# Attention probabilities sent through memory: the rearranging moved from the load to the store

## The chip, the cores and the metric

One core of a Trainium2 chip runs the whole program. The metric is the device time of one execution in microseconds, lower is better.

## What is computed

The reference is a gated block on x (4 sequences of 512 tokens, width 1024) with a context of 4 x 64 keys. First cross attention: x is normalised, queries are formed with Wq (32 heads of 128), keys and values from the context (8 key/value heads), both rotated by position, and

    attn = softmax(mask(q k^T * 128**-0.5));  x = x + tanh(g_xattn) * (attn v) Wd^T

Then a quantised feed-forward of inner width 512 (gate, up, down) with its own gate is added. Everything in the attention is float32 work; operands of TensorE are split in a high and a low part, and three products take the place of one.

The part that the change touches is the transposed copy of the probabilities: for each batch row and pair of heads, P (tokens x keys) has to become P^T (keys x tokens), so that TensorE can contract over the keys.

## The kernel before

**Tiling.** The batch is worked in two halves of two sequences. In a half there are 8 groups (one key/value head each) of 4 units; a unit is one pair of heads on one sequence, so there are 32 units in a half and 64 in all. TensorE's order is written out by hand in slots, one slot per unit (L652). In the slot of unit u it computes the queries of u in eight parts (`queries`), the scores of unit u-1 (`score`), some of the products of Wd with the values (`values`, eight per group) and some of the sixteen `outputs` of the group before, which multiply P^T (`pt_hi`, `pt_lo`) with those products (`vw_hi`, `vw_lo`). The slots of a group are called kind 0 to 3 (u modulo 4). `outputs(gg, 0)` is the first to need P^T of the group's unit of kind 2; it stands in the slot of kind 0 of the next group.

**The probabilities.** VectorE subtracts the row maximum of the scores into `prob` (L1438, `softmax_a`), ScalarE takes the exponential in place (L959), VectorE sums, scales and transposes `prob` in blocks of 32 x 32 (L1444 to L1455, `softmax_b`). After that the 32 x 32 blocks are right inside, but stand in the wrong places. For all units but the last two of each half (`moved`, L294: 30 per half, 60 in all) the blocks are put in place by a trip through memory, `move_probs` (L451), issued by the sync engine (SP):

- one store of `prob`, 128 rows of 2 KB, to one of two halves of `p_dram`, laid out (a, q, t, c, i): a is the block row and q the row in it (together the partition), t one of four token tiles, c the block column (32 keys), i the column in it;
- a wait for it (L457), and a wait until `pt_raw`, which has one buffer, was read by VectorE for the unit before (L459);
- four loads (L461), one for each c, into 32 partitions of `pt_raw` each. Memory has 32 consecutive floats for each (q, t, a), so such a load is made of 512 pieces of 128 bytes.

ScalarE copies `pt_raw` to `pt_hi` (L944, `copy_probs`) and VectorE forms `pt_lo` (L1317 with `lower_probs`, L1457). There is one `prob` buffer: the subtraction for unit u+1 waits until the store of unit u has landed (L1435).

**What stands around it on each engine.** The order on each engine is fixed. SP in the slot of kind 3, after the move of the unit of kind 2: a piece of Wd (`next_wd`, L424), then in the next slot a pair of Wq (four transfers, L358), Wd, keys, Wd, values. VectorE in a slot of kind 0: rotation of the queries before (`turn_second`), `lower_values`, `lower_probs(unit - 2)`, `softmax_a(unit - 1)`, `lower_values`, the first half of the rotation (`turn_first`, L1413, which frees the bank of PSUM that the next slot's queries need), two additions of outputs, `softmax_b(unit - 1)`. ScalarE in that slot: values, a piece of Wd, `copy_probs(unit - 2)`, `exponential(unit - 1)`, values.

Of the kernel before, what the change touches and what calls it, by code (L numbers as in the profile page):

```python
# [46 lines left out]
BT = SEQ // P  # L47
# [40 lines left out]
def gated_block(nc, x, ctx_t, g_att, g_ffn, wq_t, wk_t, wv_t, wd_t, wg_t, wu_t, wo_t,  # L88
# [4 lines left out]
    p_dram = nc.dram_tensor("p_scratch", (2, 4, 32, BT, 4, 32), F32, kind="Internal").ap()  # L93

    root = ExitStack()
    with root:
        def sem(name):
            return root.enter_context(nc.semaphore(name))

        def sb(stack, name, shape, dt):  # L100
            return stack.enter_context(nc.sbuf_tensor(name, [P] + shape, dt))
# [38 lines left out]
        with ExitStack() as s:  # L140
# [8 lines left out]
            prob = sb(s, "prob", [2 * BT, KEYS], F32)  # L149
# [18 lines left out]
            pt_raw = sb(s, "pt_raw", [BT, 4, 32], F32)  # L168
# [62 lines left out]
        turned_done, p_out = sem("turned_done"), sem("p_out")  # L231
        pt_in = [sem("pt_in0"), sem("pt_in1")]
# [61 lines left out]
        def moved(unit):  # L294

            return unit % UNITS < UNITS - 2

        def moves(unit):

            return unit + 1 - 2 * (unit // UNITS)  # L300

        def turns(unit):

            return unit % UNITS - (UNITS - 2) + 1 + 2 * (unit // UNITS)
# [24 lines left out]
        def _(sp):  # L329
# [121 lines left out]
            def move_probs(unit):  # L451

                n = moves(unit)
                sp.wait_ge(turned_done, n)
                sp.dma_start(p_dram[n % 2, :, :, :, :, :].rearrange("a q t c i -> (a q) (t c i)"),
                             prob[:, :, :].rearrange("p s k -> p (s k)")).then_inc(p_out, 16)
                sp.wait_ge(p_out, 16 * n)  # L457
                if unit:
                    sp.wait_ge(pt_lo_done, unit)  # L459
                for c in range(4):  # L460
                    sp.dma_start(pt_raw[32 * c:32 * c + 32, :, :, :],  # L461
                                 p_dram[n % 2, :, :, :, c, :].rearrange("a q t i -> q t a i")).then_inc(pt_in[n % 2], 16)

            load_k(0)
            load_v(0)
            for half in range(HALVES):
                for u in range(UNITS):
                    unit, gg = half * UNITS + u, half * GROUPS + u // UPG
                    if u % 2 == 0 and 1 < unit // 2 + 1 < HALVES * PAIRS and unit != UNITS:
                        sp.wait_ge(q_done, unit)  # L470
                        load_wq(unit // 2 + 1)
                    if u % UPG == 0 and u >= UPG:
                        next_wd(VPG * gg - 2)
                        next_heads(gg)
                        next_wd(VPG * gg - 1)
                        next_values(gg)
                    if u % UPG == 1 and half == 0:
                        sp.wait_ge(part_done, HTILES + u // UPG)
                        sp.dma_start(xn[:, :], x[HTILES + u // UPG, :, :]).then_inc(xs_in, 16)
                    if u % UPG == 2:  # L480
                        next_wd(VPG * gg)
                        next_wd(VPG * gg + 1)
                    if u % UPG == 3:
                        for i in range(2, 5):
                            next_wd(VPG * gg + i)
                    if u >= 1 and moved(unit - 1):
                        move_probs(unit - 1)
                    if u % UPG == 3:
                        next_wd(VPG * gg + 5)
                    if half == 1 and 1 <= u <= 5:  # L490
                        load_again(((0, 1), (2, 3), (4,), (5, 6), (7,))[u - 1])
# [391 lines left out]
        def _(act):  # L883
# [50 lines left out]
            def copy_probs(unit):  # L934
                p, b, gg = (unit // HB) % 2, unit % HB, unit // UPG
                if gg >= 1:
                    act.wait_ge(o_ps, (gg - 1) * OPG + (b + 1) * 2 * BT)
                if moved(unit):
                    act.wait_ge(pt_in[moves(unit) % 2], 64 * ((moves(unit) + 1) // 2))
                    src = pt_raw[:, :, :, :].rearrange("p t a i -> p (t a i)")  # L940
                else:
                    act.wait_ge(pt_ps, turns(unit))
                    src = p_turned
                act.activation(pt_hi[:, p, b, :], src, ACT.Copy).then_inc(pt_hi_done, 1)  # L944
# [20 lines left out]
            def slot(half, u):  # L965
                unit, gg, kind, filled = half * UNITS + u, half * GROUPS + u // UPG, u % UPG, u >= UPG
                if kind == 0 and filled:
                    copy_values(gg - 1, 6)
                    split_wd(VPG * gg - 1)
                    copy_probs(unit - 2)  # L970
                    exponential(unit - 1)
                    copy_values(gg - 1, 7)
                    next_wq(unit, 0)
                    next_wq(unit, 1)
                    split_wd(VPG * gg)
# [9 lines left out]
                if kind == 1:  # L985
                    if unit > 1:
                        split_wd(VPG * gg + 1)
                        split_wd(VPG * gg + 2)
                    if filled:
                        copy_probs(unit - 2)  # L990
                    exponential(unit - 1)
                    next_wq(unit, 2)
                    next_wq(unit, 3)
                if kind == 2:
                    copy_probs(unit - 2)
                    exponential(unit - 1)
                    copy_values(gg, 0)
                    next_wq(unit, 0)
                    copy_values(gg, 1)
                    next_wq(unit, 1)  # L1000
# [312 lines left out]
        def _(dve):  # L1313
# [110 lines left out]
            def softmax_a(unit):  # L1424

                dve.wait_ge(s_done, unit + 1)
                view = scores[:, 0:P].rearrange("p (h k) -> p h k", h=2)
                dve.tensor_tensor(view, view, cst[:, C_MASK:C_MASK + KEYS].unsqueeze(1).broadcast_to([P, 2, KEYS]),  # L1428
                                  ALU.add).then_inc(mask_done, 1)
                dve.wait_ge(mask_done, unit + 1)  # L1430
                view = scores.rearrange("p (s k) -> p s k", k=KEYS)
                dve.tensor_reduce(red[:, 0, :], view, AX_X, ALU.max).then_inc(max_done, 1)
                dve.wait_ge(max_done, unit + 1)
                if unit and moved(unit - 1):
                    dve.wait_ge(p_out, 16 * moves(unit - 1))  # L1435
                elif unit:
                    dve.wait_ge(pt_ps, turns(unit - 1))
                dve.tensor_tensor(prob[:, :, :], view, red[:, 0, :].unsqueeze(2).broadcast_to([P, 2 * BT, KEYS]),  # L1438
                                  ALU.subtract).then_inc(sub_done, 1)
# [58 lines left out]
            def slot(half, u):  # L1498
                unit, gg, kind, filled = half * UNITS + u, half * GROUPS + u // UPG, u % UPG, u >= UPG
                if kind == 0:  # L1500
                    if filled:
                        turn_second(unit - 1)
                        lower_values(gg - 1, 6)
                        lower_probs(unit - 2)
                        softmax_a(unit - 1)
                        lower_values(gg - 1, 7)
                    else:
                        for t in range(BT, BT + 2):
                            lower_rows(half, t)
                    turn_first(unit)  # L1510
                    if not filled:
                        for t in range(BT + 2, HTILES):
                            lower_rows(half, t)
                    if filled:
                        add(gg - 1, 0)
                        add(gg - 1, 1)
                        softmax_b(unit - 1)
                if kind == 1:
                    turn_second(unit - 1)
                    if filled:  # L1520
                        add(gg - 1, 2)
                        add(gg - 1, 3)
                        add(gg - 1, 4)
                    softmax_a(unit - 1)
                    turn_first(unit)
                    if filled:
                        lower_probs(unit - 2)
                        add(gg - 1, 5)
                    softmax_b(unit - 1)
                    if filled:  # L1530
                        add(gg - 1, 6)
                        add(gg - 1, 7)
                    if half == 0:
                        dve.wait_ge(xs_in, 16 * (u // UPG + 1))
                        statistics(HTILES + u // UPG, xn[:, :])
# [282 lines left out]
```

## Time and profile before

| what | us |
|---|---|
| time, median of 3 runs | 1502.36 (1499.65 to 1502.42) |
| the profiled execution, its own time | 1503.76 |
| its span in the profile | 1502.0 |
| TensorE matmul busy | 1431.9 (95% of the span) |
| VectorE busy | 1021.5 (68%) |
| ScalarE busy | 562.9 (37%) |
| GpSimd busy | 611.3 (41%) |

The time of a run holds the span and a little around it (1.8 us here). PE is TensorE's matmuls, PEld its weight loads, DVE VectorE, ACT ScalarE, POOL GpSimd, SPq the sync engine's queue of transfers. A row of a timeline has the start, the duration, the engine, the line and what is written from what; in square brackets stands how long the engine was idle before it and what ended that. In a row of DMA issues the last number is the median time from issue to landing.

### The profile page before, as it was taken

The numbers are of one execution on the slowest core, as the hardware profiler recorded it, in microseconds if no ns is written. First come the engines' busy times: TensorE is split into PE (matmuls) and PEld (weight loads), VectorE is DVE, ScalarE is ACT, GpSimd is POOL, SyncE is SP. The second block draws the span as 40 slices with busy tenths as digits, with TensorE's granted clock in tenths as the row PEclk, the third lists the DMA queues.
The fourth block names the chain that finished last, engine by engine and source line by source line (L and its number), as shares of the span: only waits on it lengthen the run. The fifth ranks groups of instructions, "written<-read, shape, count | busy, mean of one in ns | idle before, by whom it ended". The sixth has DMA issues, their size and how long they took to land.

```text
span 1502.0 us, 19112 instructions
## 1 busy us (share of the span) xinstructions
PE 1431.9 (95%) x7235; PEld 1169.7 (78%) x7248; DVE 1021.5 (68%) x1578; ACT 562.9 (37%) x863; POOL 611.3 (41%) x415
## 2 busy tenths in 40 slices
PE   7899999999999999998999999999999999987886
PEld 7778888888888888886878888888888888874443
DVE  5967575757576767667465757575666666677997
ACT  4424141414142423244542424232323223248985
POOL 3535252434343443430343434334344334334674
PEclk9999999999999999999999999999999999998999
DMA  8834343433425242438255242423333333473655
GB/s 298 244 79 116 75 112 73 108 84 87 105 70 122 61 115 73 105 80 264 65 145 141 74 104 62 102 71 91 80 93 78 93 85 93 100 223 127 127 116 96
DMA packets 327131, 166.52 MB, mean 111 GB/s; under 512 B 275200, under 2 KB 290048, under 8 KB 326656
## 3 DMA queue, kind: packets, MB, share of 16 engines
q1 hardware_dynamic: 324448, 154.29, 38.8%
q0 software_dynamic: 2592, 11.01, 4.5%
q8 instruction: 58, 0.95, 0.3%
q14 instruction: 33, 0.27, 0.1%
HBM read 132.74 MB, written 35.65 MB: 112 GB/s over the span
## 4 chain that ended last, share of the span: by engine, by line
PE 75%; DVE 13%; DMA 3%; ACT 2%; issue 2%; POOL 2%; SPq 2%; POOLq 0%; ACTq 0%; DVEq 0%
PE psum L558 15%; PE psum L560 15%; PE psum L559 15%; PE psum L612 7%; PE psum L647 7%; PE psum L648 7%; PE psum L649 7%; DVE psum L1577 2%; DVE vw_lo L1317 1%; DVE xg L1583 1%; DVE res L1621 1%; DMA wv_raw<-in_wv_t 1%; SPq L358 1%; POOL rot L1208 1%; DMA wd_raw<-in_wd_t 1%
## 5 line engine op out<-in xcount | busy, mean ns | idle before, releaser
L558 PE MATMUL psum<-xt_hi,wq_hi 128*128 128x512 f32 x1024 | 402.3, 393 | 2.0 <-DVE xt_lo L1317 2.0
L560 PE MATMUL psum<-xt_hi,wq_lo 128*128 128x512 f32 x1024 | 399.4, 390 | 0.0
L559 PE MATMUL psum<-xt_lo,wq_hi 128*128 128x512 f32 x1024 | 399.2, 390 | 0.0
L1180 POOL TENSOR_TENSOR wq_lo<-wq_raw,wq_hi 128x512 fp32r<-128x512 f32 x128 | 170.8, 1345 | 495.0 <-ACT wq_hi L909 495.0
L1478 DVE TENSOR_TENSOR acc<-psum,acc 128x512 f32<-128x512 f32 x224 | 151.5, 681 | 138.2 <-PE psum L649 138.2
L1208 POOL TENSOR_TENSOR rot<-rot 128x1024 f32<-128x1024 f32 x64 | 153.5, 2398 | 214.0 <-DVE rot L1421 213.2
L558 PEld LDWEIGHTS psum<-xt_hi,wq_hi 128*128 128x128 f32 x1024 | 192.9, 188 | 42.3 <-DVE xt_lo L1317 2.8
L560 PEld LDWEIGHTS psum<-xt_hi,wq_lo 128*128 128x128 f32 x1024 | 192.6, 188 | 40.5
L955 ACT ACTIVATE vw_hi<-psum 64x512 fp32r<-64x512 f32 x256 | 151.4, 591 | 193.6 <-PE psum L560 190.0
L559 PEld LDWEIGHTS psum<-xt_lo,wq_hi 128*128 128x128 f32 x1024 | 192.9, 188 | 39.3
L1317 DVE TENSOR_TENSOR vw_lo<-psum,vw_hi 64x512 fp32r<-64x512 f32 x256 | 175.8, 687 | 54.2 <-ACT vw_hi L955 48.0
L647 PE MATMUL psum<-vw_hi,pt_hi 128*128 128x512 f32 x512 | 203.5, 398 | 7.6 <-DVE acc L1481 3.9
L649 PE MATMUL psum<-vw_hi,pt_lo 128*128 128x512 f32 x512 | 199.5, 390 | 0.0
L648 PE MATMUL psum<-vw_lo,pt_hi 128*128 128x512 f32 x512 | 199.4, 390 | 0.0
L1180 POOL TENSOR_TENSOR wd_lo<-wd_raw,wd_hi 128x512 fp32r<-128x512 f32 x128 | 170.8, 1341 | 68.2 <-ACT wd_hi L914 68.2
L944 ACT ACTIVATE pt_hi<-pt_raw 128x512 fp32r<-128x512 f32 x60 | 37.7, 628 | 283.3 <-DMA pt_raw<-p_scratch 282.3
L959 ACT ACTIVATE prob<-prob 128x512 f32<-128x512 f32 x64 | 40.4, 632 | 259.1 <-DVE prob L1438 259.1
L612 PEld LDWEIGHTS psum<-kblk,rot 128*128 128x128 f32 x1024 | 122.8, 191 | 12.0 <-issue 8.3
L612 PE MATMUL psum<-kblk,rot 128*128 128x128 f32 x1024 | 125.6, 276 | 3.2 <-POOL rot L1208 3.2
L1428 DVE TENSOR_TENSOR psum<-psum,cst 128x128 f32<-128x128 f32 x64 | 19.2, 299 | 154.0 <-PE psum L612 153.5
L647 PEld LDWEIGHTS psum<-vw_hi,pt_hi 128*128 128x128 f32 x512 | 96.2, 188 | 30.5 <-DVE pt_lo L1317 5.0
L649 PEld LDWEIGHTS psum<-vw_hi,pt_lo 128*128 128x128 f32 x512 | 96.1, 188 | 20.2
(148 smaller groups left out, 1920.4 us busy)
## 6 DMA issues: line engine op xcount, KB each, us to landing
wq_raw<-in_wq_t SPq DMA_DIRECT2D x128, 256.0 KB, 4.3
wd_raw<-in_wd_t SPq DMA_DIRECT2D x128, 256.0 KB, 3.7
p_scratch<-prob SPq DMA_DIRECT2D x60, 256.0 KB, 2.0
pt_raw<-p_scratch SPq DMA_DIRECT2D x240, 64.0 KB, 2.5
acc<-in_x SPq DMA_DIRECT2D x16, 512.0 KB, 4.9
out_x<-acc SPq DMA_DIRECT2D x16, 512.0 KB, 4.1
xa<-out_x SPq DMA_DIRECT2D x16, 512.0 KB, 3.8
out_x<-res POOLq DMA_DIRECT2D x15, 512.0 KB, 5.5
```

Source lines behind the costliest of these rows:

```text
L558: pe.matmul(dst, a_hi, b_hi, start=start, stop=False)
L559: pe.matmul(dst, a_hi, b_lo, start=False, stop=False)
L560: return pe.matmul(dst, a_lo, b_hi, start=False, stop=stop)
L612: ins = pe.matmul(scores[:, t * P:(t + 1) * P], rot[:, 0, j, t * P:(t + 1) * P], kblk[:, j, 2 * b:2 * b + 2, :].rearrange("p a k -> p (a k ...
L647: pe.matmul(dst, p_hi, vw_hi[:, p, b, cols], start=(p == 0), stop=False)
L648: pe.matmul(dst, p_hi, vw_lo[:, p, b, cols], start=False, stop=False)
L649: ins = pe.matmul(dst, p_lo, vw_hi[:, p, b, cols], start=False, stop=(p == 1))
L955: act.activation(vw_hi[rows, p, bl, cols], bank(V_BANK + i % 2)[rows, :], ACT.Copy).then_inc(vw_hi_done, 1)
L1180: pool.tensor_tensor(dst, full, hi.bitcast(F32), ALU.subtract).then_inc(done, 1)
L1208: pool.tensor_tensor(rot[:, 0, :, :], rot[:, 0, :, :], rot[:, 1, :, :], ALU.add).then_inc(rope_done, 1)
L1317: dve.tensor_tensor(dst, full, hi.bitcast(F32), ALU.subtract).then_inc(done, 1)
L1478: dve.tensor_tensor(acc[:, tile, cols], bank(O_BANK + c % 2), acc[:, tile, cols], ALU.add).then_inc(o_done, 1)
```

## The change

The rearranging moves from the load to the store. `p_dram` keeps its shape (2, 4, 32, 4, 4, 32), but is now read as (c, q, t, a, i). Four stores, one for each c, take the 32 columns of c of every token tile of `prob` (128 partitions x 4 tiles x 128 bytes) and put each piece at its place (a outermost on both sides, then q and t); one load then takes 128 whole rows of 2 KB into `pt_raw`. The thresholds on the two semaphores follow: `p_out` counts 64 per unit in place of 16, `pt_in` 16 in place of 64.

```diff
                 n = moves(unit)
                 sp.wait_ge(turned_done, n)
-                sp.dma_start(p_dram[n % 2, :, :, :, :, :].rearrange("a q t c i -> (a q) (t c i)"),
-                             prob[:, :, :].rearrange("p s k -> p (s k)")).then_inc(p_out, 16)
-                sp.wait_ge(p_out, 16 * n)
+                for c in range(4):
+                    sp.dma_start(p_dram[n % 2, c, :, :, :, :].rearrange("q t a i -> a q t i"),
+                                 prob[:, :, :].rearrange("p s k -> p (s k)").rearrange("p (t c i) -> p t c i", t=BT, c=4)[:, :, c, :]).then_inc(p_out, 16)
+                sp.wait_ge(p_out, 64 * n)
                 if unit:
                     sp.wait_ge(pt_lo_done, unit)
-                for c in range(4):
-                    sp.dma_start(pt_raw[32 * c:32 * c + 32, :, :, :],
-                                 p_dram[n % 2, :, :, :, c, :].rearrange("a q t i -> q t a i")).then_inc(pt_in[n % 2], 16)
+                sp.dma_start(pt_raw[:, :, :, :].rearrange("p t a i -> p (t a i)"),
+                             p_dram[n % 2, :, :, :, :, :].rearrange("c q t a i -> (c q) (t a i)")).then_inc(pt_in[n % 2], 16)
...
                 if moved(unit):
-                    act.wait_ge(pt_in[moves(unit) % 2], 64 * ((moves(unit) + 1) // 2))
+                    act.wait_ge(pt_in[moves(unit) % 2], 16 * ((moves(unit) + 1) // 2))
...
                 if unit and moved(unit - 1):
-                    dve.wait_ge(p_out, 16 * moves(unit - 1))
+                    dve.wait_ge(p_out, 64 * moves(unit - 1))
```

## Rows read from the trace of the kernel before

**Rows 1.** The page: busy time of TensorE, and its granted clock in 40 slices.
```profile
PE 1431.9 (95%) x7235; PEld 1169.7 (78%) x7248; DVE 1021.5 (68%) x1578; ACT 562.9 (37%) x863; POOL 611.3 (41%) x415
...
PEclk9999999999999999999999999999999999998999
```

**Rows 2.** Who waited for whom: us in total, times, longest.
```profile
ACT pt_hi L944 <- DMA pt_raw<-p_scratch: 282.3, 44, 10.6
...
DVE pt_lo L1317 <- ACT pt_hi L944: 41.7, 17, 3.7
...
PE psum L647 <- DVE pt_lo L1317: 3.6, 4, 1.5
PE psum L558 <- POOL wd_lo L1180: 3.4, 1, 3.4
```

**Rows 3.** The page: DMA issues, KB each, median us from issue to landing.
```profile
wd_raw<-in_wd_t SPq DMA_DIRECT2D x128, 256.0 KB, 3.7
p_scratch<-prob SPq DMA_DIRECT2D x60, 256.0 KB, 2.0
pt_raw<-p_scratch SPq DMA_DIRECT2D x240, 64.0 KB, 2.5
```

**Rows 4.** Timeline of SP's queue, 519 to 540 us: the move of unit 22 (kind 2).
```profile
521.06 0.33 SPq L455 DMA_DIRECT2D p_scratch<-prob  x1
523.04 2.60 SPq L461 DMA_DIRECT2D pt_raw<-p_scratch  x4
525.68 0.62 SPq L364 DMA_DIRECT2D wd_raw<-in_wd_t  x1
```

**Rows 5.** Timelines of DVE and ACT, same stretch.
```profile
520.32 0.71 DVE L1455 STREAM_TRANSPOSE prob<-prob 128x512 f32<-128x512 f32 x1
...
528.36 0.69 DVE L1317 TENSOR_TENSOR pt_lo<-pt_raw,pt_hi 128x512 fp32r<-128x512 f32 x1 [2.60 <-ACT pt_hi L944]
...
530.14 0.69 DVE L1438 TENSOR_TENSOR prob<-psum,red 128x512 f32<-128x512 f32 x1
532.15 1.41 DVE L1317 TENSOR_TENSOR vw_lo<-psum,vw_hi 64x512 fp32r<-64x512 f32 x2 [1.32 <-ACT vw_hi L955]
533.48 1.21 DVE L1413 TENSOR_TENSOR rot<-psum,cst 128x1024 f32<-128x1024 f32 x1
...
527.70 0.63 ACT L944 ACTIVATE pt_hi<-pt_raw 128x512 fp32r<-128x512 f32 x1 [2.10 <-DMA pt_raw<-p_scratch]
```

**Rows 6.** Timeline of TensorE: first use of that P^T, first queries of next slot.
```profile
531.50 0.39 PE L647 MATMUL psum<-vw_hi,pt_hi 128*128 128x512 f32 x1
...
536.95 0.39 PE L558 MATMUL psum<-xt_hi,wq_hi 128*128 128x512 f32 x1
```

**Rows 7.** DMA, 539 to 542 us (store of unit 23, issued 539.09): 40 slices, packets.
```profile
DMA  0000000000004999999973000000000000000000
...
DMA packets 144, 0.26 MB, mean 87 GB/s; under 512 B 16, under 2 KB 16, under 8 KB 144
...
q1 hardware_dynamic: 144, 0.26, 22.6%
```

**Rows 8.** DMA, 541.9 to 544.6 us: only pieces of 128 bytes of L461.
```profile
q1 hardware_dynamic: 1600, 0.20, 46.9%
```

**Rows 9.** Landing of wd_raw, 575 to 600 us.
```profile
DMA to landing us min/median/max: 2.9/3.2/4.1
```

**Rows 10.** SP's queue and ACT at the second half's start: units 32 and 33.
```profile
740.64 0.33 SPq L455 DMA_DIRECT2D p_scratch<-prob  x1
...
753.83 0.43 SPq L455 DMA_DIRECT2D p_scratch<-prob  x1
760.31 2.67 SPq L461 DMA_DIRECT2D pt_raw<-p_scratch  x4
763.08 1.04 SPq L445 DMA_DIRECT2D acc<-in_x  x2
...
769.56 0.63 ACT L914 ACTIVATE wd_hi<-wd_raw 128x512 fp32r<-128x512 f32 x1 [5.24 <-DMA wd_raw<-in_wd_t]
```

**Rows 11.** Unit 25 (kind 1), a piece of Wd behind the move: SP, ACT, PE.
```profile
577.84 0.43 SPq L455 DMA_DIRECT2D p_scratch<-prob  x1
...
588.10 0.63 ACT L914 ACTIVATE wd_hi<-wd_raw 128x512 fp32r<-128x512 f32 x1 [1.27 <-DMA wd_raw<-in_wd_t]
...
592.66 0.39 PE L558 MATMUL psum<-wd_hi,v_t 128*128 128x512 f32 x1
```

## The prediction

> **What bounds the kernel now.** I read the page first. TensorE is busy 95% of the span at the higher of its two clock levels (2.4 GHz) nearly throughout [rows 1], so time is gained or lost only where TensorE comes to stand still or stops doing so. The table of waits says how much of that the probabilities cause today: 3.6 us in all for `pt_lo` [rows 2]. ScalarE waits 282.3 us for `pt_raw`, but mostly ahead of its work. The one place where that wait is passed on is VectorE's 41.7 us for `pt_hi`, in 17 waits [rows 2]. The timelines tell where: VectorE takes `pt_lo` of a unit of kind 2 at once when it is there, in all 14 groups that have such a unit moved (7 per half). Unit 22 stands for them. I measure from T = 521.03, the end of its transposition (520.32 + 0.71) [rows 5]. The store is issued at T+0.03, the first load at T+2.0, the fourth ends its issue at T+4.6 [rows 4], `pt_hi` starts at T+6.7, and `pt_lo` is ready at 529.05, T+8.0 [rows 5]. TensorE needs it at 531.50, T+10.5 [rows 6]. **The slack is 2.45 us**, and that is what the change has to fit in.
>
> **Bytes and issues.** Nothing changes in the sum: 256 KB out, 256 KB in, 2048 pieces of 128 bytes once, 128 rows of 2 KB once, five issues for five. Four issues with 512 pieces cost SP 2.6 us, one with whole rows 0.33 us [rows 4], before and after; I cost them at nothing in total. What changes is the order: the long part now comes ahead of the wait at L457, and ahead of the release of `prob`. The thresholds of semaphores cost nothing.
>
> **Price of the store.** A piece of 128 bytes takes an engine 46.9% x 16 x 2.7 us / 1600 = 12.7 ns [rows 8]; a row of 2 KB takes 22.6% x 16 x 3 / 128 = 85 ns [rows 7]. These are loads into SBUF and stores of whole rows; no row shows pieces of 128 bytes written to memory, and none shows a transfer whose outermost count is below 32. So two prices have to be bounded. First, how many engines share a store. The old one has 128 rows outermost and fills all 16 (slices at 9 tenths) [rows 7]. The new one has a outermost in memory, with a count of 4, against 128 partitions. Spread over 16 engines, each has 32 pieces of a store, 0.4 us; if the work is cut along the outermost index, only 4 engines can have a share, each 128 pieces of a store and 512 of the four: 512 x 12.7 ns = 6.5 us. I take 4 engines, since the outermost count is the only thing in which these stores leave the pattern of the rows. (The Trainium skill, DMA: Bandwidth & Descriptors, section on why a DMA increments its semaphore by 16, says the same: the engines used are the largest number up to 16 that divides the outermost size of both sides. By it 128 and 4 give 4; no run here shows it yet.) Second, the price of a piece: between 12.7 ns and, with a read ahead of each write, twice that; I take 12.7, the nearest row.
>
> **The move with 4 engines.** The old store was issued at 539.09, its packets run from slice 13 to 22 of 0.075 us (539.9 to 540.65), and the first load is issued at 541.08: 0.8 us ahead of the data, 0.43 behind. The new stores are all landed at T + 0.03 + 0.8 + 6.5 + 0.45 = T+7.8, where it was T+2.0. Then one load of 128 x 2 KB, for which the twin is a piece of Wd: 2.9 to 4.1 us, median 3.2 [rows 9], 3.7 over the span [rows 3]. At best it is 2.0, as for the old store [rows 3]. With 3.2, `pt_hi` starts at T+11.0, 4.3 us later than now.
>
> **What that does in a group.** `pt_lo` of unit 22 would be ready at 533.35, TensorE wants it at 531.50: a stall of 4.3 - 2.45 = 1.85 us. Behind it on VectorE stand the softmax of the next unit, `vw_lo` and the rotation L1413, which TensorE needs for the next slot's queries at 536.95 [rows 6]. Late by 4.3 us, but without the idle 1.32 us there [rows 5] and with the exponential and two copies of ScalarE in between, it ends at 538.95, against 536.95 + 1.85 = 538.8: another 0.15. In sum **2.0 us x 14 = 28 us**. The next unit's probabilities then come some 3 us late, against TensorE's 2, and their own move again 4.3 us later; by the same timelines P^T of kinds 3, 0 and 1 is wanted by VectorE at T+12.2, T+24.3 and T+17.8, and they absorb it. The wait for `prob` also fits: landed at T+7.8, wanted at 530.14, T+9.1 [rows 5].
>
> **SP's queue.** Behind the move SP is free at T+8.2 where it was T+4.65, 3.5 us later. In the steady state this is covered. The tightest is the piece of Wd behind the move of kind 1: stores issued at 577.84, landed at 585.65, Wd issued at 586.0 and landed 3.2 to 4.1 later, high and low part made by ScalarE (0.63) and GpSimd (1.3): ready at 591.1 to 592.1, wanted at 592.66 [rows 11]. Without that cover it would cost up to 2 us per group. At the start of a half there is none: TensorE already waits 3.4 us for `wd_lo` [rows 2], because ScalarE waits 5.24 us for the Wd behind the move of unit 33 [rows 10]. That store would be issued 3.5 us later (unit 32 pushes it), land at 757.3 + 7.8 = 765.1, and the Wd goes out at 766.6 instead of 764.1: 2.5 us. For units 0 and 1 I take 3.5. Together **6 us**.
>
> **Sum.** The profiled execution took 1503.76 us, 1.4 above the median. 1503.76 + 28 + 6 = 1537.8, against the median **1536 us**, 2.3% slower. With the load at 2.0 us the stall is 0.65 in place of 1.85, the rotation is in time, and the half starts give 4: +13, 1516 us.
>
> **Rival 1: all 16 engines share the stores; no change.** The last store is issued at T+2.0, lands 2.5 us later [rows 3] at T+4.5, the load at T+7.7: 1.0 us late against a slack of 2.45. SP is as free as now. Behind unit 33 the move even costs 2.3 us less after the wait at 760.31 (one issue for four) [rows 10], which could give back 2 of the 3.4 us of rows 2. Time 1500 to 1503. For it: all transfers of the trace are spread like that. Against it: none has a count of 4 outermost. It decides if the outermost count does not limit the spread.
>
> **Rival 2: small writes to memory cost twice.** A piece costs 25.4 ns, the stores land at T+14.3, P^T at T+17.5; the group stalls 10.8 - 2.45 + 0.15 = 8.5 us, 14 times 119 us. From 15.3 ns on, `prob` is late too ((9.1 - 1.25) / 512), and VectorE stops at L1438. The half starts give 6 + 2 x 6.5 = 19. Time 1503 + 138 = 1640. Each ns above 12.7 costs 0.51 us x 16 = 8.2 us, so half as much again (19 ns) gives 1588. For it: the price is of reads, the writes are unseen. Against it: rows of 2 KB cost a store 85 ns, and the 12.7 ns are small already for their size. (The Trainium skill, DMA: Bandwidth & Descriptors, Specifications, says that below 512 bytes an SDMA engine does a read-modify-write. It gives no price; the loads of 128 bytes here show none.)
>
> **How the numbers follow.** Forecast (4 engines, 12.7 to 15 ns): 0.50, 1516 to 1555. Rival 2, with all prices above that: 0.30. Rival 1: 0.15, nearly all of it within 0.2% (3 us, about what a measurement of this kernel can tell from no change). The rest, 0.05, goes to slower in ways not costed. The range reaches down to rival 1 (1501) and up to 18 to 20 ns per piece (1595); left out is what lies near the double price. Of rival 1, 0.02 goes to faster and 0.13 to no change. Faster 0.02, same 0.13, slower 0.85.
>
> **What would show it.** Step by step in the changed profile: during the stores a DMA share of about a quarter for some 6.5 us, where rival 1 has bursts near 0.4; landing of `p_scratch` up to 7 us for the last of four; the load issued at T+7.8; `pt_hi` of kind 2 at T+11; TensorE's wait for `pt_lo` up from 3.6 to about 30 us, in 14 or more waits; a longer wait for `wd_lo` at the start of each half. The forecast is wrong if the share is spread (then no change), if the load goes out at T+14 (then rival 2), or if TensorE stands still behind Wd in every group.

## The result, and the profile after

The changed kernel takes **1542.78 us** (median of 4 runs, 1539.23 to 1544.98) where the kernel before, run beside it, takes 1502.39 us (1499.65 to 1502.88). The ratio is 1.0264, with a 95% interval of 1.0249 to 1.0279. The forecast was 1536 us in a range of 1501 to 1595. The profiled execution of the changed kernel took 1539.23 us, the shortest of the four, and that of the kernel before 1503.76 us, so two traces are compared below that lie 35.5 us apart, where the medians lie 40.4 apart: the traces leave some 5 us of the loss unplaced.

The page of the changed kernel, its span, busy times, packets and DMA issues, against [rows 1, 3]:

```profile
span 1537.4 us, 19125 instructions
...
PE 1442.3 (94%) x7248; PEld 1166.8 (76%) x7248; DVE 1024.9 (67%) x1578; ACT 561.3 (37%) x863; POOL 612.7 (40%) x415
...
PEclk9999999999999999999999999999999999999999
...
DMA packets 324251, 166.51 MB, mean 108 GB/s; under 512 B 272320, under 2 KB 287168, under 8 KB 323776
...
p_scratch<-prob SPq DMA_DIRECT2D x240, 64.0 KB
pt_raw<-p_scratch SPq DMA_DIRECT2D x60, 256.0 KB, 2.6
```

The bytes and the instructions are the same. TensorE's busy time reads 10.4 us more; about 5 us of that are 13 matmuls whose records the trace of the kernel before lacks (7235 for 7248, 0.39 us each). The span grew by 35.4 us. The packets are a fingerprint. The page of the kernel before:

```profile
DMA packets 327131, 166.52 MB, mean 111 GB/s; under 512 B 275200, under 2 KB 290048, under 8 KB 326656
```

The changed one has 2880 fewer, which is 12 for each of the 240 stores. A store of the kernel before has 144 packets for 128 rows, 16 of them under 512 B [rows 7]; I read these as one small packet to the semaphore from each engine that takes part, and they are what is missing. The window around the move of unit 22 shows it directly. The DMA view, 536.6 to 542.8 us (40 slices), and behind it the rates of the old store, 539 to 542 us (the window of [rows 7]):

```profile
DMA  0012333333333334443333443444433444444330
GB/s 0 0 23 41 55 55 55 55 55 55 51 55 55 55 53 44 44 45 42 42 45 43 44 45 42 44 44 44 42 43 44 45 44 43 44 44 44 42 33 0
DMA packets 2064, 0.26 MB, mean 42 GB/s; under 512 B 2064, under 2 KB 2064, under 8 KB 2064
...
q1 hardware_dynamic: 2064, 0.26, 34.3%
```

```profile
GB/s 0 0 0 0 0 0 0 0 0 0 0 0 191 382 437 437 382 410 437 437 273 110 0 0 0 0 0 0 0 0 0 0 0 0 0 0 0 0 0 0
```

2064 packets are 2048 pieces and 16 for semaphores, that is 4 for each of the four stores; the old store had 144 for 128 rows, 16 for itself. So 4 engines share a store, and they move 42 to 55 GB/s for 5.7 us, where the old one reached 437 GB/s. (The Trainium skill, DMA: Bandwidth & Descriptors, on the semaphore increment of 16, gives the largest number up to 16 that divides both outermost sizes; for 128 and 4 the trace agrees, with 4 packets.)

The timelines of SP, ACT, DVE and PE for the same move, against [rows 4 to 6]:

```profile
535.04 0.71 DVE L1455 STREAM_TRANSPOSE prob<-prob 128x512 f32<-128x512 f32 x1
...
535.78 4.17 SPq L456 DMA_DIRECT2D p_scratch<-prob  x4
543.42 0.33 SPq L461 DMA_DIRECT2D pt_raw<-p_scratch  x1
...
546.20 0.63 ACT L944 ACTIVATE pt_hi<-pt_raw 128x512 fp32r<-128x512 f32 x1 [6.29 <-DMA pt_raw<-p_scratch]
...
546.87 0.69 DVE L1317 TENSOR_TENSOR pt_lo<-pt_raw,pt_hi 128x512 fp32r<-128x512 f32 x1 [6.78 <-ACT pt_hi L944]
...
547.61 0.50 PE L647 MATMUL psum<-vw_hi,pt_hi 128*128 128x512 f32 x1 [1.20 <-DVE pt_lo L1317]
```

With T = 535.75 the load goes out at T+7.67 (before T+2.0), `pt_hi` starts at T+10.45 (before T+6.7) and the first product with P^T starts at T+11.86 (before T+10.47). The table of waits, against [rows 2]:

```profile
ACT pt_hi L944 <- DMA pt_raw<-p_scratch: 443.6, 44, 20.1
...
DVE pt_lo L1317 <- ACT pt_hi L944: 100.2, 26, 7.4
...
PEld psum L647 <- DVE pt_lo L1317: 27.7, 18, 2.0
...
PE psum L647 <- DVE pt_lo L1317: 20.5, 18, 1.6
...
PE psum L558 <- POOL wd_lo L1180: 8.8, 2, 6.2
...
PEld psum L558 <- DVE rot L1413: 4.3, 14, 0.3
```

Four waits of TensorE for `pt_lo` became 18. The four old ones stand at the ends of the halves (678 and 698, 1328 and 1345 us in the kernel before); the 14 new ones are one for each group with a moved unit of kind 2. Behind each of these is a wait of 0.3 us for the rotation L1413, and VectorE's wait grew by 58.5 us. The transpositions of the units of kind 2 are a good ruler for where the rest went. Before, they end (start plus 0.71) at 131.08, 209.03, 599.00, 777.28 and 1248.42 us for units 2, 6, 26, 34 and 58; after, at 134.55, 214.63, 615.84, 799.65 and 1282.95. So 3.5 us are lost ahead of unit 2, 13.4 in the six groups to unit 26 (2.2 each), 5.5 in the last group and the start of the second half, 12.2 in the six groups to unit 58 (2.0 each), and 0.9 behind it. Together these are the 35.4 us of the span.

### The profile page after: what moved, and what is told of

Read it like the earlier page. It is cut to its first block, busy times and chain, and to the rows that moved or that the text cites. A ratio compares the mean times of both kernels' runs of the same rounds, so it can differ in the third digit from the quotient of the medians.

```text
span 1537.4 us, 19125 instructions
## 1 busy us (share of the span) xinstructions
PE 1442.3 (94%) x7248; PEld 1166.8 (76%) x7248; DVE 1024.9 (67%) x1578; ACT 561.3 (37%) x863; POOL 612.7 (40%) x415
## 4 chain that ended last, share of the span: by engine, by line
PE 60%; DVE 18%; DMA 11%; SPq 4%; ACT 3%; issue 2%; POOL 1%; ACTq 0%; POOLq 0%; DVEq 0%
PE psum L558 11%; PE psum L559 11%; PE psum L560 11%; PE psum L647 8%; PE psum L648 7%; PE psum L649 7%; PE psum L612 5%; DMA p_scratch<-prob 5%; SPq L456 3%; DMA pt_raw<-p_scratch 3%; DVE psum L1577 2%; DVE pt_lo L1317 2%; DVE vw_lo L1317 2%; DVE rot L1413 1%; DVE xg L1583 1%
## 5 line engine op out<-in xcount | busy, mean ns | idle before, releaser
L1180 POOL TENSOR_TENSOR wq_lo<-wq_raw,wq_hi 128x512 fp32r<-128x512 f32 x128 | 167.1, 1317 | 540.0 <-ACT wq_hi L909 540.0
L647 PE MATMUL psum<-vw_hi,pt_hi 128*128 128x512 f32 x512 | 206.3, 403 | 24.4 <-DVE pt_lo L1317 20.5
L1180 POOL TENSOR_TENSOR wd_lo<-wd_raw,wd_hi 128x512 fp32r<-128x512 f32 x128 | 175.7, 1379 | 95.4 <-ACT wd_hi L914 95.4
L1317 DVE TENSOR_TENSOR pt_lo<-pt_raw,pt_hi 128x512 fp32r<-128x512 f32 x60 | 66.9, 1114 | 99.9 <-ACT pt_hi L944 99.3
L914 ACT ACTIVATE wd_hi<-wd_raw 128x512 fp32r<-128x512 f32 x128 | 78.8, 626 | 96.8 <-DMA wd_raw<-in_wd_t 95.9
```

Source lines behind the costliest of these rows:

```text
L647: pe.matmul(dst, p_hi, vw_hi[:, p, b, cols], start=(p == 0), stop=False)
L1180: pool.tensor_tensor(dst, full, hi.bitcast(F32), ALU.subtract).then_inc(done, 1)
L1317: dve.tensor_tensor(dst, full, hi.bitcast(F32), ALU.subtract).then_inc(done, 1)
```

## The experiments

All times of experiments are medians; where there is no interval, there was one run. Ratios are to the kernel before, run beside them (1501.97 us beside runs 1 to 4, 1502.60 beside 5 and 6, 1502.11 beside 7).

**1. Stores by block row.** The same 4 issues, 2048 pieces and one load, but the stores are cut so that 32 partitions stand outermost on one side and q with t, 128, on the other.

```diff
-                for c in range(4):
-                    sp.dma_start(p_dram[n % 2, c, :, :, :, :].rearrange("q t a i -> a q t i"),
-                                 ... [:, :, c, :]).then_inc(p_out, 16)
+                for a in range(4):
+                    sp.dma_start(p_dram[n % 2, :, :, :, a, :].rearrange("c q t i -> q t c i"),
+                                 prob[32 * a:32 * a + 32, :, :] ... "p (t c i) -> p t c i").then_inc(p_out, 16)
```

> The four stores are cut by block row a (32 partitions each, memory side with q and t outermost, 128) instead of by block column c; the number of issues (4), pieces (512 each, 128 bytes) and the one load stay as in the changed kernel. Theory A (only 4 engines share a store whose outermost count is 4): now 16 share it, the load goes out at T+4.5 in place of T+7.7, pt_hi of kind 2 starts at T+7.3, inside the slack of 2.45 us; time 1500 to 1503, TensorE's wait for pt_lo back to about 4 us. Theory B (pieces of 128 bytes written to memory go at some 340 per us in all, whatever number of engines): load still at T+7.7, time 1543.

Measured: **1497.53 us** (12 runs), ratio to the kernel before 0.9968 (0.9956 to 0.9981). It beats both kernels, the one before by 0.3%. Timelines of SP and ACT, unit 22 (T = 521.28), and then the DMA view, 521 to 526 us:

```profile
521.31 2.60 SPq L456 DMA_DIRECT2D p_scratch<-prob  x4
525.45 0.33 SPq L461 DMA_DIRECT2D pt_raw<-p_scratch  x1
...
528.14 0.63 ACT L944 ACTIVATE pt_hi<-pt_raw 128x512 fp32r<-128x512 f32 x1 [2.29 <-DMA pt_raw<-p_scratch]
```

```profile
DMA packets 2112, 0.26 MB, mean 52 GB/s; under 512 B 2112, under 2 KB 2112, under 8 KB 2112
...
q1 hardware_dynamic: 2112, 0.26, 30.3%
```

2112 packets: 64 for semaphores, 16 per store. The load goes out at T+4.17 and `pt_hi` starts at T+6.86. A piece written to memory takes (30.3% x 16 x 5 us) / 2112 = 11.5 ns, no more than the 12.7 ns of the same piece loaded [rows 8]. Theory B, a fixed rate of small writes whatever the number of engines, falls here. (The Trainium skill, same page, Specifications, has a read-modify-write below 512 bytes; no run here separates a cost of it. Written or loaded, a small piece costs more per byte, 11.5 to 12.7 ns for 128 bytes against 85 ns for a row of 2 KB [rows 7], and writing it costs no more than loading it.)

**2. Two block rows at a time.** Eight stores with an outermost count of 2 (the thresholds on `p_out` count 128 per unit).

```diff
                 for c in range(4):
+                    for h in range(2):
+                        sp.dma_start(p_dram[n % 2, c, :, :, 2 * h:2 * h + 2, :].rearrange("q t a i -> a q t i"),
+                                     prob[64 * h:64 * h + 64, :, :] ... [:, :, c, :]).then_inc(p_out, 16)
```

> Eight stores of two block rows each (64 partitions, outermost count 2) in place of four; same pieces. Theory A: 2 engines share a store, 1024 pieces for each, at 11.8 ns 12.1 us in place of 6: the load goes out at T+13.5 to T+14.3, P^T of kind 2 is 6 us later again, and prob is late too; 14 x 6 plus 2 x 6 at the half starts on top of 1543, so 1630 to 1660. Theory B: same 340 pieces per us, load at T+7.7 to T+8, time 1543 to 1550.

Measured: 1821.15 us (one run). Timelines of SP and ACT, unit 26 (T = 736.16), the DMA view, 737 to 750 us, and then two rows of its table of waits (lines are one higher in this kernel):

```profile
736.19 10.18 SPq L457 DMA_DIRECT2D p_scratch<-prob  x8
749.78 0.33 SPq L462 DMA_DIRECT2D pt_raw<-p_scratch  x1
...
752.45 0.63 ACT L945 ACTIVATE pt_hi<-pt_raw 128x512 fp32r<-128x512 f32 x1 [14.31 <-DMA pt_raw<-p_scratch]
```

```profile
DMA packets 2065, 0.27 MB, mean 21 GB/s; under 512 B 2064, under 2 KB 2064, under 8 KB 2064
```

```profile
PE psum L648 <- DVE pt_lo L1318: 98.3, 18, 7.3
...
DVE prob L1439 <- DMA p_scratch<-prob: 68.1, 19, 7.8
```

2064 small packets are 2048 pieces and 16 more, 2 for each of the eight stores. The load goes out at T+13.62, as theory A said. The time does not follow my sum: 1630 to 1660 was priced mostly for kind 2. `pt_hi` now starts at T+16.3 to T+16.4 in kinds 0, 2 and 3 and at T+21.2 in kind 1 (medians), VectorE waits 68.1 us for `prob`, TensorE waits 40.0 us for `wd_lo` in 18 waits where the changed kernel has 2, and from unit 6 to unit 26 a group takes 98.4 us in place of 78.0. The mean granted clock of TensorE is 0.933 of full here, 0.993 in the kernel before: stretches at the lower level (1.2 GHz) add to the loss where TensorE stands still more.

**3. Whole rows, but 4 outermost.** The kernel before, with a gap in memory after each block row: one store of 128 rows of 2 KB, no small pieces written. The four loads read around the gap and are otherwise the same (their lines are left out here).

```diff
-    p_dram = nc.dram_tensor("p_scratch", (2, 4, 32, BT, 4, 32), ...
+    p_dram = nc.dram_tensor("p_scratch", (2, 4, 33, BT, 4, 32), ...
-                sp.dma_start(p_dram[n % 2, :, :, :, :, :].rearrange("a q t c i -> (a q) (t c i)"),
+                sp.dma_start(p_dram[n % 2, :, 0:32, :, :, :].rearrange("a q t c i -> a q (t c i)"),
```

> The kernel before (one store of whole rows, four loads), but the scratch in memory has a gap after each block row, so that its outermost count is 4 with 32 rows of 2 KB each. Theory A: 4 engines share it, 32 rows x 85 ns = 2.7 us in place of 0.7, the loads go out at T+4.0 in place of T+2.0, pt_hi of kind 2 at T+8.7, 2.0 us later, inside the slack of 2.45; semaphore packets fall from 16 to 4 per store; time 1502 to 1507 (the half starts may show 2 us each). Theory B: small pieces are the cost and not the outermost count, so loads at T+2.0 as before and no difference in any row.

Measured: 1552.48 us, ratio 1.0335 (1.0315 to 1.0355). The DMA view, 538.2 to 544.2 us, around the store of unit 22 (issued 538.39), and then, from SP's timeline, the first loads behind it (three together):

```profile
DMA  0000000002280230501023112222222222211000
GB/s 0 0 0 0 0 0 0 0 0 55 41 55 0 14 14 0 27 0 14 27 68 68 41 68 109 109 96 96 109 109 82 109 109 109 96 68 55 0 0 0
DMA packets 132, 0.26 MB, mean 44 GB/s; under 512 B 4, under 2 KB 4, under 8 KB 132
```

```profile
544.11 1.93 SPq L461 DMA_DIRECT2D pt_raw<-p_scratch  x3
```

4 small packets for 128 rows: the outermost count alone takes 12 of the 16 engines away, without any small piece. The rate reaches 109 GB/s, a quarter of the old store's 437. The size was off: I had 2.7 us of moving, but the flow is thin for some 1.5 us before it reaches its rate, and the loads go out at T+5.75, not T+4.0. `pt_hi` of kind 2 then starts at T+10.3 in the first half and T+11.2 in the second (medians), beyond the slack, where T+8.7 was expected. So the time missed the expected 1502 to 1507 by 45 us: the kernel loses 50.5 us, 10 more than the changed one, with 80.6 us a group in the first half and 82.0 in the second (the changed kernel has 80.2 and 80.6). The thin start is not explained.

**4 and 5. Which moves matter.** The block-row stores for the units of kind 2 only, and the reverse.

```diff
+                if unit % UPG == 2:      # run 5: != 2
+                    ...                  (four stores by block row, as in run 1)
+                else:
+                    ...                  (four stores by block column, as in the changed kernel)
```

> Stores by block row for the units of kind 2 only (14 moves), the changed kernel's stores for the other 46. Theory A with the loss at the kind 2 units: 1543 less 14 x 2.1 = 1513. Rival C (the loss is spread over all moves, by SP's queue and the Wd behind it): a quarter of the 40 us goes, 1533.

Measured: 1515.42 us, ratio 1.0088 (1.0071 to 1.0105).

> The complement of the run before: the changed kernel's stores (by block column, 4 engines) for the 14 moves of kind 2 only, stores by block row (16 engines) for the other 46. If the loss sits at kind 2: on top of 1498 (all by block row) 14 x 2.1 = 29, so 1527, and the two parts add up: 1527 + 1515 - 1498 = 1544, the changed kernel. If the late release of prob or SP's queue in the other kinds had a share, the time is below 1520.

Measured: 1524.18 us, ratio 1.0140 (1.0121 to 1.0159). TensorE's waits in run 4 and then in run 5 (lines are five higher in both kernels):

```profile
PE psum L563 <- POOL wd_lo L1185: 7.6, 2, 5.3
...
PE psum L617 <- POOL rot L1213: 6.5, 12, 1.9
...
PE psum L652 <- DVE pt_lo L1322: 3.6, 4, 1.5
```

```profile
PE psum L652 <- DVE pt_lo L1322: 22.5, 18, 1.7
```

The two add up: over the block-row kernel they lose 17.9 and 26.7 us, 44.6 together, and the changed kernel loses 45.3. So 60% of the loss sits in 14 of the 60 moves. Runs 4 and 5 came within 3 us of the 1513 and 1527 expected, and run 4 far from rival C's 1533. With kind 2 spared, the 14 waits for `pt_lo` are gone and the four old ones stay. What is left is the Wd at the start of a half and 12 short waits of the scores for the rotation (the kernel before has 5, of 3.2 us in all), a cost that my sum did not have: a group takes 78.6 us there in the first half.

**6. Four loads behind the four stores.** The lateness of P^T alone (the threshold on `pt_in` is 64 again).

```diff
-                sp.dma_start(pt_raw ... "p t a i -> p (t a i)", p_dram[n % 2, ...] ... "c q t a i -> (c q) (t a i)")
+                for c in range(4):
+                    sp.dma_start(pt_raw[32 * c:32 * c + 32, :, :, :].rearrange("p t a i -> p (t a i)"),
+                                 p_dram[n % 2, c, :, :, :, :].rearrange("q t a i -> q (t a i)")).then_inc(pt_in[n % 2], 16)
```

> The changed kernel's four stores, but four loads of 32 whole rows each in place of one of 128 rows. The first load goes out at T+7.7 as in the changed kernel, the fourth about 1.0 to 1.3 us later, and pt_hi of kind 2 starts about 1.0 us later, at T+11.4. Every us of lateness beyond the slack should cost 14 us: 1543 + 14 + 1 = 1558. If the loss did not grow with the lateness of P^T (a fixed cost of the stores), it stays at 1543.

Measured: 1572.50 us, ratio 1.0462 (1.0444 to 1.0481). TensorE's waits (lines one higher):

```profile
PE psum L648 <- DVE pt_lo L1318: 33.2, 18, 3.0
...
PE psum L613 <- POOL rot L1209: 12.1, 14, 2.4
```

`pt_hi` of kind 2 is later by 0.5 to 0.7 us in the first half (T+10.9) and by up to 1.6 in the second. The loss grows with it, but faster than I had it: 30 us, not 15. The waits for `pt_lo` grow from 20.5 to 33.2 us, and a second wait behind them, of the scores for the rotation, from 5.5 us in 10 waits to 12.1 in 14. The rest is not placed; part of it may be the clock, since the three longer of the four runs (1571.92 to 1573.61 us) have a mean granted clock of 0.982 to 0.983 of full, where the changed kernel's runs have 0.989 to 0.994. A table over the runs, first half, units 6 to 26:

| kernel | `pt_hi` of kind 2 starts at T+ | one group, us |
|---|---|---|
| before | 6.8 | 78.0 |
| stores by block row (1) | 6.9 | 78.0 |
| 4 engines for all kinds but 2 (4) | 6.9 | 78.6 |
| 4 engines for kind 2 only (5) | 10.4 | 79.8 |
| changed | 10.4 | 80.2 |
| whole rows on 4 engines (3) | 10.3 | 80.6 |
| four loads (6) | 10.9 | 81.4 |
| 2 engines (2) | 16.4 | 98.4 |

**7. A piece of Wd ahead of the wait.** Run 1 with a try at what TensorE waits for at the start of the second half.

```diff
                 sp.wait_ge(p_out, 64 * n)
+                if unit == UNITS + 1:
+                    next_wd(VPG * GROUPS + 2)
+                    next_wd(VPG * GROUPS + 3)
                 if unit:
                     sp.wait_ge(pt_lo_done, unit)
...
-                        for i in range(2, 5):
+                        for i in range(4 if unit == UNITS + 3 else 2, 5):
```

> Stores by block row as in the first experiment, and at unit 33 two pieces of Wd are issued between the landing of the stores and the wait for pt_lo, in place of behind the load. With stores by block row TensorE still waits 3.2 us for wd_lo there, and its granted clock falls to 0.66 of full for a stretch of 10 us. If SP's wait at L459 is what holds that Wd back, the wait and the low stretch go: 3 to 6 us less, 1492 to 1495. If the Wd is late for another reason (its own landing, ScalarE's order), 1497 to 1498 as without it.

Measured: 1499.33 us, ratio to the kernel before 0.9983 (0.9972 to 0.9994): no gain over run 1. The wait is still there, 3.7 us. (The expectation gives run 1 a clock of 0.66 for 10 us there; its windows show 0.83 from 760 to 770.) Timelines of PE and then SP in the kernel before tell why:

```profile
755.82 0.39 PE L558 MATMUL psum<-wd_hi,v_t 128*128 128x512 f32 x1
...
761.43 0.79 PE L558 MATMUL psum<-wd_hi,v_t 128*128 128x512 f32 x1 [3.41 <-POOL wd_lo L1180]
```

```profile
752.45 1.34 SPq L364 DMA_DIRECT2D wd_raw<-in_wd_t  x2
753.83 0.43 SPq L455 DMA_DIRECT2D p_scratch<-prob  x1
```

The wait ends at 761.43, before the Wd behind the move of unit 33 is even issued (764.17). The piece it waits for is the one issued at 752.45, ahead of that move, behind the pair of Wq and so behind the move of unit 32.

## Why the prediction was right

- **How many engines.** Right, and the step on which the rest hangs: 4, by the small packets and by runs 1, 2 and 3: the engines go 16, 4, 2 with the outermost count of small pieces, and are 4 with whole rows too. Shown. One sign that was named for it did not come: the DMA share was 0.34 and not a quarter (see the last section).
- **Price of a piece.** 12.7 ns was taken. 340 pieces per us by 4 engines (44 GB/s) are 11.8 ns each. The 12.7 was taken from the recorded times of packets; by that measure 16 engines write a piece in 11.5 ns and 4 engines in 34.3% x 16 x 6.2 us / 2064 = 16.5 ns, with packets that overlap. That the engine's rate came out at 11.8 is in part luck: the sum took packet times as if they did not overlap. Rival 2 is out. The load went out at T+7.67 against T+7.8.
- **The load.** Sized too long: 2.6 us to landing against 3.2, so P^T is 3.75 us late and not 4.3.
- **Stall of a group.** The product starts 1.39 us later against 1.85 forecast, and the next slot's queries 0.2 more (T+17.5 against T+15.9), where 0.15 was forecast. What was missed made it up: kind 2 alone costs 1.8 us a group (run 5), and the other three kinds do not absorb everything (run 4: 0.6 us a group, with waits of the scores for the rotation). Sum 2.0 to 2.2 us per group against 2.0. A right sum of two errors, a stall sized too long and a term put at nothing, and so luck in part.
- **Start of the halves.** 3.5 us ahead of unit 2 as forecast. For the second half 2.5 were forecast, and 5.5 less one group at 2.1, 3.4, came. The link named was wrong (run 7): not the Wd behind unit 33's move, but the one behind Wq and unit 32's. TensorE's wait went from 3.41 to 6.25 us:

```profile
783.80 0.80 PE L558 MATMUL psum<-wd_hi,v_t 128*128 128x512 f32 x1 [6.25 <-POOL wd_lo L1180]
```

- **The sum.** 34 us were forecast on top of the profiled execution. The traces show 35.4, the medians 40.4. So the mechanism holds, and by the medians the sum was 6 us short, of which the traces place 1.4.
- **Wd behind the move of kind 1.** No wait of TensorE for it in the steady state, as forecast: both waits for `wd_lo` stand at the start of a half (120.5 and 783.8 us).
- **Rival 1** is what run 1 makes of the change: 1497.5 us, below its 1500 to 1503. The term named there, one issue instead of four after the wait at L459, seems to be worth more than at unit 33 alone. In the first half a group takes 78.0 us in both. In the second half of the kernel before a group takes 78.5 us (777.28 to 1248.42, six groups), and with stores by block row 78.0. SP in both kernels at unit 57, and then GpSimd's wait for the high part of Wd over the second half (777 to 1249 and 776 to 1244 us), each before and then with stores by block row:

```profile
1231.32 2.66 SPq L461 DMA_DIRECT2D pt_raw<-p_scratch  x4
1234.03 1.10 SPq L364 DMA_DIRECT2D wd_raw<-in_wd_t  x2
```

```profile
1228.59 0.33 SPq L461 DMA_DIRECT2D pt_raw<-p_scratch  x1
1228.96 1.90 SPq L364 DMA_DIRECT2D wd_raw<-in_wd_t  x2
```

```profile
POOL wd_lo L1180 <- ACT wd_hi L914: 14.0, 6, 3.3
```

```profile
POOL wd_lo L1180 <- ACT wd_hi L914: 3.2, 4, 1.3
```

The Wd goes out 5.1 us earlier. Of this 3.4 are the lag of the kernel before by then (its transposition of unit 57 ends at 1223.67, that of run 1 at 1220.28) and 2.3 the issues saved, less 0.7 by which the load of run 1 goes out later behind its transposition. Behind the late Wd GpSimd reaches the rotation late: in that stretch the scores wait three times for it (1.4 us) in the kernel before, and never in run 1. Of the 5.8 us between the two traces 1.6 fall from unit 26 to unit 34, 3.2 in the six groups to unit 58 and 1.3 behind it. That the gain comes from SP's fewer issues is argued from these rows; no run isolates it.

## What to carry to other kernels

When a rearrangement by DMA can stand on the store or on the load, and can be cut in several ways, look at the outermost count of both access patterns first: here 32 or more outermost on both sides used 16 engines, 4 used 4, and 2 used 2. Count the packets under 512 B that are not data to see how many engines took part. The same bytes in the same pieces, stored by 16 engines or by 4, let the load go out 4.2 or 7.7 us behind the transposition, and gave 1497.5 or 1542.8 us. Then hold the lateness against the slack of the first consumer that is taken at once, and expect the cost beyond the slack to grow faster than that slack alone says, as in runs 2 and 6, where the waits behind it grew too.

## What the runs showed that was not expected

- A store of 512 pieces on 4 engines holds SP's queue for 1.16 us (median of 240), against 0.64 us for a load of 512 pieces on 16 and 0.63 us for a store of 512 pieces on 16 (run 1). It goes with the number of engines; why is not shown. I take it to cost nothing here, since SP waits for the landing anyway.
- The DMA share with 4 engines is 0.32 to 0.41 (stretches of 1 us from 537 to 542) and not 0.25, while the rate stays at 42 to 55 GB/s. If 4 engines move the data, as the small packets say, the recorded times of neighbouring packets overlap, so a share is no count of engines.
- Whole rows on 4 engines (run 3) begin with about 1.5 us at a thin rate, which small pieces on 4 engines do not show. Open.
- A wait of some us at the start of the second half comes with a fall of the granted clock. In the kernel before (3.41 us of wait) and in the changed one (6.25 us) the stretch of 10 us in which it ends has a granted clock of 0.66, so this is no part of the difference between them; in run 1 (3.18 us) it is 0.83 from 760 to 770 us (windows view of the first two; columns: stretch and length, busy time and instructions of PE, PEld, DVE, ACT and POOL, granted clock, DMA share, GB/s):

```profile
760.00:770.00 10.00, 8.57 (x34) 7.17 (x35) 4.45 (x8) 2.67 (x5) 6.21 (x4) 0.66 0.70 183
```

```profile
780.00:790.00 10.00, 6.20 (x19) 4.96 (x20) 6.38 (x8) 4.56 (x9) 8.10 (x6) 0.66 0.54 152
```
